# GpSimd's product with C written in place over the states, in one ring of six, and the skip one slot earlier

## The chip, the cores and the metric

The kernel runs on one core of one Trainium2 chip. The metric is the device time of one execution in microseconds (us); its time is given as the median of three runs. The engines are named PE (TensorE), DVE (VectorE), ACT (ScalarE), POOL (GpSimd) and SP (SyncE, which only issues transfers here).

## The reference, cut to what matters

The network has two layers on 16 images of 48 channels and 64 x 64 pixels. Layer 0 is a depthwise convolution with a routed expert and a feed-forward block; layer 1 masks the pixels, takes a 2D cosine transform, runs a selective scan on each of four quadrants, transforms back, and ends with a feed-forward block. The change touches the selective scan alone:

```python
xi = silu(conv(xi) + conv_b)                       # 96 channels d, 1024 positions l
delta = softplus(dt @ dt_w + dt_b)
dA = exp(delta[..., None] * A)                     # 16 states s per channel
dBu = delta[..., None] * Bm[:, :, None, :] * xi[..., None]
def step(h, inp):
    dA_t, dBu_t, C_t = inp
    h = dA_t * h + dBu_t
    return (h, jnp.einsum('bds,bs->bd', h, C_t))
y = ys + xi * Dp                                   # the skip
y = y * silu(z)                                    # the gate
out = jnp.einsum('bld,cd->blc', y, out_w)
```

(Shortened; `dt`, `Bm` and `Cm` come from `xi` by a matrix product, and `ys` are the results of `step` over the positions.)

## The kernel before

The 16 images are worked on in 8 pairs, one after the other. In a pair the scan has 8 units `v` (4 quadrants times 2 images), and a unit has 12 slots `m`. In a slot, 8 channels times 16 states make 128 partitions, and 1024 positions lie along the free axis, so a step is one instruction of 128 x 1024 on each engine. Each engine's program is written out by hand: `scan_stage` calls `step(v, m)` for a slot and then `prep(m, v + 1)`, which prepares the next unit. An engine runs its own list strictly in this order, and semaphores tie the engines together.

For slot `m` of a unit the work is:

- PE, `broadcast_u` (L625, L626): copies `u` = delta * xi to the 128 partitions in PSUM, into one of two bank pairs. It is issued one slot ahead and waits until the scan two slots back has read its banks (`h_ready`).
- ACT, `decay` (L875): dA = exp(A * delta), two slots ahead, in a ring of three (`da`).
- DVE, the mult (L1143): `driven` = broadcast u * B, in place in PSUM. Then the scan (L1148): h = dA * h + driven along the positions, from PSUM and `da` into `hs`, a ring of two. The scan waits until POOL has read the state of two slots back (`pr_ready`).
- POOL, the product (L1229): state * C from `hs` into `pr`, a ring of four (`PRS`). It waits for the scan (`h_ready`) and until PE has read the ring's slot (`y_acc`).
- PE, `states` (L644): once for three slots (a trio), six matmuls add three products into the sum y in PSUM. Trios 0, 1 and 2 are added in slots 4, 7 and 10, trio 3 in slot 1 of the next unit.

PE's list also holds, once per unit: `skip` (L636, xi * D with a diagonal matrix, which opens the sum y and so stands ahead of trio 0; it waits for the gate of the unit before, `yz_ready`) in slot `S_SKIP`; XI (L584) in slot 0, Z (L592) in slot 2, DT (L598) in slot 3, B (L604) in slot 5, C (L610) in slot 7, all for the next unit; and every second unit the output projection (L654) in slot 9. DT's result goes through five activations on ACT (the first at L842, the last, a logarithm, at L851, with a `decay` among them). DVE turns it into delta by one add of two SBUF operands (the delta add, L1125) after the scan of slot 5. POOL then multiplies u (L1218). DVE's gate (L1133) follows the scan of slot 1.

The last unit of a pair prepares nothing, so it has neither DT nor delta add.

## Time and profile before

| | us |
|---|---|
| median of 3 runs | 5493.2 |
| lowest and highest of the 3 | 5470.5 and 5499.7 |
| profiled execution | 5469.5 |
| its span, first to last instruction | 5467.7 |
| PE busy | 4310.0 (79%) |
| DVE busy | 3967.0 (73%) |
| ACT busy | 2693.4 (49%) |
| POOL busy | 2379.3 (44%) |

The mean granted clock of TensorE is 0.786 of full speed. The eight pairs look alike, each about 683 us, of which the scan takes a little under 400 us. In these DVE is nearly always busy; in the rest of a pair it is not. A share of busy time over the whole span is therefore no guide to the change: what counts is which engine ends a wait last inside the scan.

### The profile page before, as it was taken

To read this page: it belongs to the slowest core of one execution; us is meant where nothing else is said; L and a number is where in the kernel's file an instruction comes from. 1 tells how busy PE (TensorE), PEld (TensorE's weight loads), DVE (VectorE), ACT (ScalarE), POOL (GpSimd) and SP (SyncE) were. 2 spreads that over 40 slices of the span, in tenths; PEclk is the share of its full clock that TensorE was granted. 3 is DMA by queue.
4 is the path that set the end of the run, shared out by engine and by line. 5 is a ranking of instruction groups with operands and counts; after the bars stand their busy time and mean duration, and the time that the engine had idled before them with its cause. 6 is when DMAs were issued, how large, how long until landed. Compare 5 with 4: busy or idle time off the path is not lost.

```text
span 5467.7 us, 47969 instructions
## 1 busy us (share of the span) xinstructions
PE 4310.0 (79%) x13448; PEld 1540.4 (28%) x13448; DVE 3967.0 (73%) x3477; ACT 2693.4 (49%) x3114; POOL 2379.3 (44%) x1148
## 2 busy tenths in 40 slices
PE   6688776887768877688776897768977688777887
PEld 2322323223232233322333223322233222332223
DVE  6588675886758866588665886658866588675886
ACT  4554355543555535555355554555535545355453
POOL 2256332563326533265333653326633266333663
PEclk8778787787878887777877778778887778877787
DMA  1355303553036520355203552036520366204651
GB/s 34 76 141 145 79 13 77 141 144 77 13 83 144 143 73 10 91 145 135 71 10 91 145 141 67 8 89 146 145 64 8 91 152 142 64 4 101 150 142 47
DMA packets 144739, 497.37 MB, mean 91 GB/s; under 512 B 19308, under 2 KB 20056, under 8 KB 143672
## 3 DMA queue, kind: packets, MB, share of 16 engines
q1 hardware_dynamic: 130104, 456.13, 34.5%
q10 hardware_dynamic: 14336, 37.76, 2.5%
q8 instruction: 126, 2.06, 0.2%
q14 instruction: 173, 1.42, 0.1%
HBM read 418.33 MB, written 37.75 MB: 83 GB/s over the span
## 4 chain that ended last, share of the span: by engine, by line
PE 34%; issue 25%; DVE 24%; ACT 8%; POOL 6%; DMA 2%; DVEq 1%; SPq 0%; POOLq 0%; ACTq 0%
DVE arena L1148 7%; DVE ps L1143 7%; PE ps L625 6%; PE ps L644 6%; POOL arena L1229 5%; PE ps L584 5%; DVE arena L1039 3%; PE ps L489 3%; PE ps L654 3%; PE ps L437 2%; PE ps L535 2%; PE ps L430 2%; ACT arena L731 2%; PE ps L480 2%; ACT arena L709 2%
## 5 line engine op out<-in xcount | busy, mean ns | idle before, releaser
L1229 POOL TENSOR_TENSOR arena<-arena 128x1024 f32<-128x1024 f32 x768 | 1804.0, 2358 | 1317.8 <-PE ps L644 848.8
L1148 DVE TENSOR_TENSOR_SCAN arena<-arena,ps 128x1024 f32<-128x1024 f32 x768 | 1756.3, 2287 | 120.4 <-ACT arena L875 17.9
L625 PE MATMUL ps<-arena,spread 32*128 32x512 f32 x1536 | 1009.9, 748 | 455.3 <-DVE arena L1148 429.0
L875 ACT ACTIVATE arena<-arena,a_all 128x1024 f32<-128x1024 f32 x768 | 869.3, 1144 | 973.6 <-DVE arena L1148 892.4
L1143 DVE TENSOR_TENSOR ps<-ps,arena 128x1024 f32<-128x1024 f32 x768 | 931.8, 1213 | 269.3 <-PE ps L626 267.9
L626 PE MATMUL ps<-arena,spread 32*128 32x512 f32 x1536 | 979.9, 748 | 0.0
L644 PE MATMUL ps<-arena,gather 128*32 128x512 f32 x3072 | 694.6, 814 | 38.4 <-POOL arena L1229 38.4
L625 PEld LDWEIGHTS ps<-arena,spread 32*128 32x128 f32 x1536 | 261.2, 209 | 1173.8 <-DVE arena L1148 769.2
L1177 POOL TENSOR_TENSOR x<-x,arena 96x512 f32<-96x512 f32 x128 | 204.2, 1595 | 862.4 <-DVE arena L957 862.4
L584 PE MATMUL ps<-arena,w_in 96*96 96x512 f32 x512 | 312.4, 767 | 63.0 <-DMA arena<-xq 63.0
L644 PEld LDWEIGHTS ps<-arena,gather 128*32 128x32 f32 x3072 | 126.5, 136 | 579.1 <-issue 528.8
L515 PE MATMUL ps<-arena 96*96 96x512 f32 x384 | 198.5, 666 | 69.7 <-DVE arena L1025 69.7
L626 PEld LDWEIGHTS ps<-arena,spread 32*128 32x128 f32 x1536 | 250.9, 208 | 0.0
L437 PE MATMUL ps<-arena,average 96*96 96x512 f32 x384 | 222.8, 664 | 29.7 <-ACT arena L702 29.7
L1125 DVE TENSOR_TENSOR arena<-arena 96x1024 f32<-96x1024 f32 x64 | 79.1, 1237 | 219.6 <-ACT arena L851 219.6
L636 PE MATMUL ps<-arena,dskip 96*96 96x512 f32 x256 | 229.8, 1051 | 0.0
L1218 POOL TENSOR_TENSOR arena<-arena 96x1024 f32<-96x1024 f32 x64 | 151.2, 2362 | 167.2 <-DVE arena L1125 167.2
L1039 DVE SCALAR_TENSOR_TENSOR arena<-arena,sel_small 96x512 f32<-96x512 f32 x192 | 217.1, 1131 | 6.6 <-DVE arena L1025 2.1
L469 PE MATMUL ps<-arena,w 128*96 128x512 fp8e5 x384 | 120.8, 429 | 125.5 <-DVE arena L932 113.0
L598 PE MATMUL ps<-arena,wdt_all 96*96 96x512 f32 x256 | 207.3, 957 | 5.5 <-ACT arena L834 5.5
L1190 POOL TENSOR_TENSOR arena<-arena 96x512 f32<-96x512 f32 x64 | 92.6, 1446 | 245.2 <-ACT arena L767 245.2
L731 ACT ACTIVATE arena<-ps 128x1536 f16<-128x1536 f32 x128 | 183.8, 1436 | 26.6 <-PE ps L459 26.6
(151 smaller groups left out, 5566.7 us busy)
## 6 DMA issues: line engine op xcount, KB each, us to landing
arena<-dl SPq DMA_DIRECT2D x768, 512.0 KB, 4.8
dl<-arena ACTq DMA_DIRECT2D x64, 384.0 KB, 3.0
xq<-in_x SPq DMA_DIRECT2D x8, 1536.0 KB, 8.8
arena<-xq SPq DMA_DIRECT2D x64, 192.0 KB, 7.4
arena<-arena ACTq DMA_DIRECT2D x64, 192.0 KB, 3.7
out<-x SPq DMA_DIRECT2D x64, 192.0 KB, 2.1
arena<-xq SPq DMA_DIRECT2D x64, 191.8 KB, 6.5
arena<-in_w SPq DMA_DIRECT2D x2, 288.0 KB
```

The lines of the kernel that those rows point to most:

```text
L437: pe.matmul(ps[0:R, depth + j % depth, :], average[:], sq[:, j % depth, :], start=True, stop=True).then_inc(averaged, 1)
L584: mm = pe.matmul(ps[0:DI, 6 + c, :], w_in[:, q, j, :], xs[:, i, c * 512 + 2 * j:c * 512 + 2 * j + 512], start=(j == 0), stop=(j == 1))
L625: pe.matmul(ps[:, bank, :], spread[rows[0], r, :], u[rows[0], i, 0:512], start=True, stop=True)
L626: mm = pe.matmul(ps[:, bank + 1, :], spread[rows[1], r, :], u_low[rows[1], i, :], start=True, stop=True)
L636: pe.matmul(ps[0:DI, c, :], dskip[:, q, :], xi[:, i, c * 512:(c + 1) * 512], start=True, stop=False, skip_group_check=True)
L644: mm = pe.matmul(ps[b * BLK:(b + 1) * BLK, c, :], gather[:, r, :], pr[:, (r * TRIO + b) % PRS, c * 512:(c + 1) * 512], start=False, stop=( ...
L731: act.activation(hf[:, j % 2, :], ps[:, 4:7, :].rearrange("p b n -> p (b n)"), ACT.Copy).then_inc(hf_ready, 1)
L875: act.activation(da[:, m % DAS, :], dbc[:, m % DBC, :], ACT.Exp, scale=a_all[:, v // 2, m:m + 1]).then_inc(da_ready, 1)
L1039: dve.scalar_tensor_tensor(out=image(acc), in0=tap_source(t, k), scalar=sel_small[:, k:k + 1], in1=image(acc), op0=ALU.mult, op1=ALU.add). ...
L1143: dve.tensor_tensor(driven, driven, bmat[:, v % 2, :], ALU.mult).then_inc(bu_ready, 1)
L1148: dve.tensor_tensor_scan(hs[:, m % 2, :], da[:, m % DAS, :], driven, 0.0, ALU.mult, ALU.add).then_inc(h_ready, 1)
L1229: pool.tensor_tensor(pr[:, m % PRS, :], hs[:, m % 2, :], cmat[:, v % 2, :], ALU.mult).then_inc(pr_ready, 1)
```

## The change

The ring `pr` is gone and `hs` has six slots (the same space as two and four before). POOL multiplies the state by C in place. PE's `states` reads its three products from `hs`. POOL no longer waits for PE; DVE's scan, which now must not overwrite a product that PE has still to read, waits for the trio that holds the slot six steps back (`y_acc`) in place of POOL's product two steps back. Apart from this, `S_SKIP` goes from 4 to 3, so `skip` stands in slot 3, ahead of DT, and not in slot 4.

```diff
--- before.py
+++ after.py
@@ -50,14 +50,14 @@
 TRIO = 3
 DBC = 3
 DAS = 3
-PRS = 4
+HSS = 6
 XSW = L + 2
 PE_XI, PE_Z, PE_DT, PE_B, PE_C = 0, 2, 3, 5, 7
 ACT_SILU, ACT_DT, ACT_SOFT, ACT_B, ACT_DL, ACT_C, ACT_U = 1, 3, 4, 6, 6, 8, 8
 DVE_DELTA = 5
 POOL_U = 5
 SP_SHIFT = 5
-S_GATE, S_SKIP, S_OUT = 1, 4, 9
+S_GATE, S_SKIP, S_OUT = 1, 3, 9
 ACT_TAPS, DVE_TAPS, PE_TAPS = (0, 1, 2), (3, 4, 5), (6, 7, 8)
 LN_DEPTH = 4
 ARENA = 30300
@@ -186,8 +186,7 @@
         u_low = cut(128, 2 * 512).rearrange("p (i n) -> p i n", i=2)
         dbc = cut(128, DBC * L).rearrange("p (b n) -> p b n", b=DBC)
         da = cut(128, DAS * L).rearrange("p (b n) -> p b n", b=DAS)
-        hs = two_of(cut(128, 2 * L))
-        pr = cut(128, PRS * L).rearrange("p (b n) -> p b n", b=PRS)
+        hs = cut(128, HSS * L).rearrange("p (b n) -> p b n", b=HSS)
         assert top[0] <= ARENA, top[0]
 
         ps = ctx.enter_context(nc.psum_tensor("ps", [128, 8, 512], F32))
@@ -642,7 +641,7 @@
                     for c in range(2):
                         for b in range(TRIO):
                             mm = pe.matmul(ps[b * BLK:(b + 1) * BLK, c, :], gather[:, r, :],
-                                           pr[:, (r * TRIO + b) % PRS, c * 512:(c + 1) * 512],
+                                           hs[:, (r * TRIO + b) % HSS, c * 512:(c + 1) * 512],
                                            start=False, stop=(r == GPB - 1), skip_group_check=True)
                     mm.then_inc(y_acc, 1)
 
@@ -1142,10 +1141,10 @@
                     dve.wait_ge(ubc_ready, n + 1)
                     dve.tensor_tensor(driven, driven, bmat[:, v % 2, :], ALU.mult).then_inc(bu_ready, 1)
                     dve.wait_ge(da_ready, n + 1)
-                    if v or m >= 2:
-                        dve.wait_ge(pr_ready, n - 1)
+                    if v or m >= HSS:
+                        dve.wait_ge(y_acc, V * GPB + (m - HSS) // TRIO + 1)
                     dve.wait_ge(bu_ready, n + 1)
-                    dve.tensor_tensor_scan(hs[:, m % 2, :], da[:, m % DAS, :], driven, 0.0,
+                    dve.tensor_tensor_scan(hs[:, m % HSS, :], da[:, m % DAS, :], driven, 0.0,
                                            ALU.mult, ALU.add).then_inc(h_ready, 1)
                     if m == S_GATE and v:
                         gate(v - 1)
@@ -1224,9 +1223,8 @@
                     if m == 0:
                         pool.wait_ge(c_ready, V + 1)
                     pool.wait_ge(h_ready, n + 1)
-                    if v or m >= PRS:
-                        pool.wait_ge(y_acc, V * GPB + (m - PRS) // TRIO + 1)
-                    pool.tensor_tensor(pr[:, m % PRS, :], hs[:, m % 2, :], cmat[:, v % 2, :],
+                    product = hs[:, m % HSS, :]
+                    pool.tensor_tensor(product, product, cmat[:, v % 2, :],
                                        ALU.mult).then_inc(pr_ready, 1)
 
                 scan_stage(prep, lambda: None, step, lambda: None)
```

PE's list at slots 3 to 5 of a unit, from broadcast 4 to broadcast 6, where `spread` is the broadcast, `wdt_all` DT, `dskip` the skip and `gather` states of trio 0. Before:

```order
L625 MATMUL ps<-arena,spread 128x512 [waits h_ready]
L626 MATMUL ps<-arena,spread 128x512
L598 MATMUL ps<-arena,wdt_all 96x512 [waits sz_ready]
L598 MATMUL ps<-arena,wdt_all 96x512
L623 REGISTER_ALU
L625 MATMUL ps<-arena,spread 128x512 [waits h_ready]
L626 MATMUL ps<-arena,spread 128x512
L636 MATMUL ps<-arena,dskip 96x512 [waits yz_ready]
L636 MATMUL ps<-arena,dskip 96x512
L641 ISA
L644 MATMUL ps<-arena,gather 32x512 [waits pr_ready]
L644 MATMUL ps<-arena,gather 32x512 x5
```

The same place after the change:

```order
L624 MATMUL ps<-arena,spread 128x512 [waits h_ready]
L625 MATMUL ps<-arena,spread 128x512
L635 MATMUL ps<-arena,dskip 96x512 [waits yz_ready]
L635 MATMUL ps<-arena,dskip 96x512
L597 MATMUL ps<-arena,wdt_all 96x512 [waits sz_ready]
L597 MATMUL ps<-arena,wdt_all 96x512
L622 REGISTER_ALU
L624 MATMUL ps<-arena,spread 128x512 [waits h_ready]
L625 MATMUL ps<-arena,spread 128x512
L640 ISA
L643 MATMUL ps<-arena,gather 32x512 [waits pr_ready]
L643 MATMUL ps<-arena,gather 32x512 x5
```

The two skip matmuls have moved ahead of DT and of broadcast 5; the rest stands as it did, and the next row in both lists is broadcast 6.

DVE's list around slots 5 and 6, with the mult, the scan (printed as SCALAR_TENSOR_TENSOR) and between them the delta add. Before:

```order
L1143 TENSOR_TENSOR ps<-ps,arena 128x1024 [waits ubc_ready]
L1148 SCALAR_TENSOR_TENSOR arena<-arena,ps 128x1024 [waits bu_ready,pr_ready,da_ready]
L1124 ISA
L1125 TENSOR_TENSOR arena<-arena 96x1024 [waits soft_act]
L1142 REGISTER_ALU
L1143 TENSOR_TENSOR ps<-ps,arena 128x1024 [waits ubc_ready]
L1148 SCALAR_TENSOR_TENSOR arena<-arena,ps 128x1024 [waits bu_ready,pr_ready,da_ready]
```

After:

```order
L1142 TENSOR_TENSOR ps<-ps,arena 128x1024 [waits ubc_ready]
L1147 SCALAR_TENSOR_TENSOR arena<-arena,ps 128x1024 [waits bu_ready,y_acc,da_ready]
L1123 ISA
L1124 TENSOR_TENSOR arena<-arena 96x1024 [waits soft_act]
L1141 REGISTER_ALU
L1142 TENSOR_TENSOR ps<-ps,arena 128x1024 [waits ubc_ready]
L1145 REGISTER_ALU [waits da_ready]
L1147 SCALAR_TENSOR_TENSOR arena<-arena,ps 128x1024 [waits bu_ready,y_acc]
```

The scan waits for `y_acc` in place of `pr_ready`. At some scans, 23 in a pair's list in place of 7, a register instruction now stands ahead of the scan and carries one of its waits. No other engine's list differs, but POOL's, where the products lose their wait for `y_acc`.

## Rows read from the trace of the kernel before

**Rows 1.** Page, costliest groups; then the scan's line, its idle time behind POOL.

```profile
L1229 POOL TENSOR_TENSOR arena<-arena 128x1024 f32<-128x1024 f32 x768 | 1804.0, 2358 | 1317.8 <-PE ps L644 848.8
L1143 DVE TENSOR_TENSOR ps<-ps,arena 128x1024 f32<-128x1024 f32 x768 | 931.8, 1213 | 269.3 <-PE ps L626 267.9
...
  POOL arena L1229: 11.0, 54
```

**Rows 2.** Timeline of DVE, second unit of the third pair (start, length).

```profile
1649.54 2.29 DVE L1148 TENSOR_TENSOR_SCAN arena<-arena,ps 128x1024 f32<-128x1024 f32 x1
...
1659.14 1.23 DVE L1143 TENSOR_TENSOR ps<-ps,arena 128x1024 f32<-128x1024 f32 x1 [0.23 <-PE ps L626]
1660.51 2.29 DVE L1148 TENSOR_TENSOR_SCAN arena<-arena,ps 128x1024 f32<-128x1024 f32 x1
1662.71 1.20 DVE L1125 TENSOR_TENSOR arena<-arena 96x1024 f32<-96x1024 f32 x1
1667.39 1.23 DVE L1143 TENSOR_TENSOR ps<-ps,arena 128x1024 f32<-128x1024 f32 x1 [3.48 <-PE ps L626]
1668.83 2.29 DVE L1148 TENSOR_TENSOR_SCAN arena<-arena,ps 128x1024 f32<-128x1024 f32 x1 [0.21 <-POOL arena L1229]
```

**Rows 3.** Timeline of PE, same unit, first row of each group.

```profile
1651.88 0.69 PE L625 MATMUL ps<-arena,spread 32*128 32x512 f32 x1 [1.94 <-DVE arena L1148]
...
1653.36 3.73 PE L598 MATMUL ps<-arena,wdt_all 96*96 96x512 f32 x4
1657.02 1.22 PE L625 MATMUL ps<-arena,spread 32*128 32x512 f32 x1
...
1659.03 3.73 PE L636 MATMUL ps<-arena,dskip 96*96 96x512 f32 x4
1662.68 3.60 PE L644 MATMUL ps<-arena,gather 128*32 128x512 f32 x12
```

**Rows 4.** Timelines of POOL and ACT, same unit.

```profile
1651.91 2.36 POOL L1229 TENSOR_TENSOR arena<-arena 128x1024 f32<-128x1024 f32 x1 [2.40 <-DVE arena L1148]
...
1657.13 1.11 ACT L842 ACTIVATE arena<-ps,small_all 96x1024 f32<-96x1024 f32 x1 [3.06 <-PE ps L598]
...
1661.25 1.15 ACT L851 ACTIVATE arena<-arena,eps 96x1024 f32<-96x1024 f32 x1
```

**Rows 5.** Windows, same unit: busy by engine, then granted clock, DMA share, GB/s.

```profile
1656.00:1666.00 10.00, 10.00 (x22) 2.05 (x20) 7.41 (x5) 7.32 (x7) 1.79 (x1) 0.50 0.88 190
```

**Rows 6.** Timelines of DVE and PE, fourth unit of the same pair.

```profile
1751.05 2.29 DVE L1148 TENSOR_TENSOR_SCAN arena<-arena,ps 128x1024 f32<-128x1024 f32 x1
...
1763.40 2.74 PE L644 MATMUL ps<-arena,gather 128*32 128x512 f32 x12
...
1767.24 1.23 DVE L1143 TENSOR_TENSOR ps<-ps,arena 128x1024 f32<-128x1024 f32 x1 [2.17 <-PE ps L626]
```

**Rows 7.** Timelines of DVE and POOL, delta adds of two units at full speed.

```profile
1615.08 1.45 DVE L1125 TENSOR_TENSOR arena<-arena 96x1024 f32<-96x1024 f32 x1
1616.46 1.22 DVE L1143 TENSOR_TENSOR ps<-ps,arena 128x1024 f32<-128x1024 f32 x1
...
5210.74 5.66 POOL L1229 TENSOR_TENSOR arena<-arena 128x1024 f32<-128x1024 f32 x2 [3.68 <-PE ps L644]
5211.63 2.56 DVE L1125 TENSOR_TENSOR arena<-arena 96x1024 f32<-96x1024 f32 x1
```

**Rows 8.** Timelines: first and last wait at slot 6; broadcast 5 of the last.

```profile
255.43 1.23 DVE L1143 TENSOR_TENSOR ps<-ps,arena 128x1024 f32<-128x1024 f32 x1 [2.33 <-PE ps L626]
...
5354.66 1.22 PE L625 MATMUL ps<-arena,spread 32*128 32x512 f32 x1 [1.47 <-DVE arena L1148]
...
5364.53 1.23 DVE L1143 TENSOR_TENSOR ps<-ps,arena 128x1024 f32<-128x1024 f32 x1 [2.84 <-PE ps L626]
```

**Rows 9.** Timelines of DVE and POOL, end of the third pair's scan.

```profile
1984.03 2.29 DVE L1148 TENSOR_TENSOR_SCAN arena<-arena,ps 128x1024 f32<-128x1024 f32 x1
1984.42 4.64 POOL L1229 TENSOR_TENSOR arena<-arena 128x1024 f32<-128x1024 f32 x2 [2.77 <-PE ps L644]
```

## Prediction

> **What bounds the kernel now.** I read the groups of instructions first. The change touches two of them: POOL's product (L1229), which stands idle 848.8 us behind PE's `states` (L644), and DVE's `mult` (L1143), which stands idle 267.9 us behind PE's `broadcast_u` (L626) [rows 1]. Which of the two idle times matters is settled by DVE's timeline of one unit [rows 2]. A step of DVE is one mult and one scan. Inside the step nothing is left over, and in the whole scan stage DVE only stops where PE or a unit's start stops it. The stops are concentrated: of the 267.9 us, 158.7 us fall on the mult of slot 6, in 59 of 64 units (the first and the last of the 59 are in [rows 8]; the sum is over all of them). POOL's idle time costs nothing by itself: the one place where DVE waits for a product is the scan of slot 6, 0.21 us of idle in [rows 2], 54 times, 11.0 us in all [rows 1].
>
> So the question is what delays slot 6, and PE's timeline of the same unit answers it [rows 3]. From 1651.88 on PE never pauses: broadcast 4, DT, broadcast 5, skip, states 0, broadcast 6. The granted clock in this stretch is 0.50, the lower level of 1.2 GHz [rows 5], after a slot in which PE was idle 1.94 us [rows 3]. PE is therefore the bound between broadcast 4 and broadcast 6, and DVE is the bound everywhere else. POOL's product 4 waits here for states 0, because its slot in the ring of four is still being read: waits of this kind make up the 848.8 us of [rows 1].
>
> **The change part by part.** *The ring.* DVE's scan now waits for `y_acc` of the trio six steps back in place of POOL's product two steps back. Slot 6 waits for states 0, but its mult already needs broadcast 6, which PE issues behind states 0 (order rows of PE). The same holds at slots 9, 0 and 3. The new wait can never end last, so it costs 0. What it gives is the scan of slot 6. Its start comes 1.44 us after a mult that itself waited; the scan of slot 5 in the same unit starts 1.37 us after such a mult [rows 2]. That is 0.07 us, 54 times: -4 us. At the end of a pair the scan of the last slot starts at 1984.03 and POOL's last two products run as one piece from 1984.42 to 1989.06 [rows 9]. A product starts 2.37 us after its scan's start when nothing else holds it (1649.54 to 1651.91 [rows 2, 4]) and takes 2.36 us [rows 4], so the last one would end at 1988.76: -0.3 us on the path to the last gate, eight times, -3 us with rounding. Sixteen more register instructions per pair stand on DVE between mult and scan. One stands ahead of almost every mult already and the delta add starts 2.20 us after a scan of 2.29 us [rows 2]: they hide behind the running instruction, 0. An in-place product reads and writes what it did; I take its 2.36 us unchanged, and even 1.1 us more would fit into the 3.5 us of a step: 0.
>
> *The skip.* It takes 3.73 us at the low clock [rows 3] and moves ahead of DT and broadcast 5. PE's total is unchanged, but broadcast 5 now ends where states 0 starts today. Mult 5 follows 0.11 us later (1659.03 to 1659.14 [rows 2, 3]). From mult 5 DVE needs 1.37 us to scan 5, 2.20 us to the delta add [rows 2] and 1.13 us to mult 6 (an add takes 1.20 us and the next mult starts 0.07 us before its end: 1615.08 + 1.45 against 1616.46 [rows 7]). So mult 6 cannot start before (start of states today) + 0.11 + 4.70 us. Today the wait at mult 6 has mult 5, scan 5 and the add running beneath it; after the change they stand behind the wait. This is the step on which the forecast rests. I went through all 64 units with it.
> - 24 units like the one in [rows 2, 3]: 1662.68 + 4.81 = 1667.49 against 1667.39. This one loses 0.1, their mean is 0.3 us: +7.
> - 27 units like the one in [rows 6], where PE was back at full speed within states 0 (2.74 us in place of 3.60): 1763.40 + 4.81 = 1768.21 against 1767.24, +0.97, mean 1.0: +27 as the lower bound. In these the clock rose right behind a skip, with the first matmuls of states. In the new order DT and broadcast 5 stand ahead of states, and in none of the 64 units does it rise on broadcasts. If the rise is as late as in the first group, mult 6 comes where it does there, 17.85 us after scan 2 starts, not 16.19 [rows 2, 6]: +1.7 each, +45, the upper bound. Nearer the upper one, 1.35: +36.
> - 5 units at or near full speed: mult 6 hardly waits today. DT comes one skip later and the delta add may be late (rival 1): between -0.3 (today's 1.45 us of the add falls to 1.20 [rows 7]) and +2.3 each (2.5 us less that 0.25), middle: +5.
> - 8 last units of a pair, without DT and delta add. PE idles 1.47 us ahead of broadcast 5, which the skip now fills, out of a wait of 2.84 us at mult 6 [rows 8]: -1.4 each if the clock stays, -0.7 if states run wholly at 3.6 us. I take -1: -8.
>
> Sum: +7 + 36 + 5 - 8 - 4 - 3 = **+33 us**. The profiled execution took 5469.5 us, so 5502 us for such a one. It lies 24 us under the median of the runs shown, 5493.2; on the median the forecast is **5526 us**.
>
> **Rivals.** *1. The delta add loses to POOL's product (slower still).* Today product 5 waits behind product 4 for states 0, so the delta add of slot 5 mostly runs alone. In the full-speed units it doesn't, and there it takes 1.45 us, once 2.56 us in place of 1.20, while the two products around it take 5.66 us in place of 4.7 [rows 7]: whichever starts second waits for the other to end. After the change product 5 becomes ready 0.17 us behind the add's turn (2.37 against 2.20 us after scan 5 starts [rows 2, 4]). The add must be ready by then. Its logarithm ends 5.27 us after DT's first evaluation starts, 0.31 us before the add [rows 2, 4]; both hang on DT and broadcast 5, so at the low clock the 0.31 us stay. If broadcast 5 runs at full speed right behind DT, it ends 1 us sooner: the add isn't ready, the product goes first and the add comes 0.17 + 2.36 = 2.5 us later. In a third of the 51 units of the first two kinds that is 17 x 2.5 = +43 us: 5569; in all of them +128: 5654. The point where it decides is 0.31 + 0.17 us of slack. The Trainium skill, "SBUF — State Buffer", section "Who interferes with whom", states the rule behind it: a VectorE instruction with two SBUF inputs contends with a GpSimd instruction that reads SBUF, and the one that issued first blocks the other for its whole length. The mult and the scan have one input in PSUM and are clear of it by that page. Trace and rule agree: the scans take 2.29 us beside a product (1984.03) and without one (1660.51) [rows 2, 9].
>
> *2. Nothing changes.* PE's work between broadcasts 4 and 6 is the same sum, and if the stop only changes its place the time stays within 10 us: 5493. For it: mult 6 moves by 0.1 us in the unit of [rows 2]. Against it: [rows 6].
>
> *3. PE keeps its full speed (faster).* The skip fills PE's idle time between broadcast 4 and broadcast 5. If the clock then stayed up as in the five full-speed units, today's wait at mult 6 would go: 3.48 us in the one kind of unit, 2.17 us in the other [rows 2, 6], 2.8 us on the mean of the 51. In half of them that is -71 us, with the +33 us falling away by half: 5493 + 17 - 71 = 5439. It decides when more than about 17 of the 51 do so. Against it: the clock falls on what PE did before broadcast 4, which the change leaves alone, and a fast broadcast 5 runs into rival 1.
>
> *4. The change does not do what it says* is out: the order rows show both parts.
>
> **How the numbers follow.** Forecast (stop moves ahead of mult 5, 5505 to 5545): 0.60. Rival 1 in a third of the units or more (5550 to 5650): 0.17. Rival 2 (5483 to 5503): 0.13. Rival 3: 0.10. A difference under 0.5%, 27 us, is about what a measurement of this kernel can't tell from none (the three runs shown spread by 29 us). The edge stands at 5521: six tenths of the forecast's chance lie above it. Slower 0.36 + 0.17 = 0.53; same 0.24 + 0.13 = 0.37; faster 0.10. The range leaves out 0.10 below and the far half of rival 1: 5480 to 5580.
>
> **What would show it.** Idle before the mult of slot 6 falls from 158.7 us to near 40 us, and a new idle of 2 to 4 us stands before the mult of slot 5 in some 50 units, 180 us or more in all. POOL's product no longer waits for states at all, and the scan never waits for POOL. The unit grows by 0 to 2 us from scan 2 to mult 6. If rival 1 holds, the delta add (L1124 after) has a mean above 1.5 us or waits for ACT outside the pair's start. If rival 3 holds, the granted clock of the span rises above 0.79. The forecast is wrong if the idle before slots 5 and 6 together falls, or if the clock's low stretches end inside DT rather than states.

## The result, and the profile after

The changed kernel takes **5549.95 us** (median of 4 runs, 5540.98 to 5567.24) against 5487.2 us for the kernel before in the same comparison (4 runs, 5470.54 to 5499.65). The ratio is 1.0115, 95% interval 1.0085 to 1.0146: 63 us slower. The forecast was +33 us. The profiled execution took 5567.24 us, with a span of 5565.4 us against 5467.7. That is the slowest of the four runs after, and the profiled execution of before, 5469.5 us, lies 18 us under its median. So sums read from the two traces account for 98 us, 35 more than the medians differ by.

First the groups of the page, as in [rows 1].

```profile
L1227 POOL TENSOR_TENSOR arena<-arena 128x1024 f32<-128x1024 f32 x768 | 1807.5, 2354 | 1401.0 <-DVE arena L1147 1401.0
L1147 DVE TENSOR_TENSOR_SCAN arena<-arena,ps 128x1024 f32<-128x1024 f32 x768 | 1755.8, 2286 | 107.4 <-ACT arena L874 13.3
...
L1142 DVE TENSOR_TENSOR ps<-ps,arena 128x1024 f32<-128x1024 f32 x768 | 932.2, 1214 | 284.5 <-PE ps L625 282.6
...
L1124 DVE TENSOR_TENSOR arena<-arena 96x1024 f32<-96x1024 f32 x64 | 173.4, 2710 | 251.3 <-ACT arena L850 251.3
```

The product costs what it did (2354 ns against 2358), and no longer waits for PE at all. The scan's wait for POOL is gone. DVE's wait for broadcasts is hardly changed as a sum, 282.6 us against 267.9. What is new stands in the last row: the delta add has a mean of 2.71 us, where the kernel before had 1.24 us (79.1 us busy in 64), and it waits 251.3 us for the logarithm, of which 217.9 us are the eight adds at the pairs' starts, as before (219.6).

DVE's timeline shows it in the fifth unit of the third pair. 46 of the 56 units with such an add look like it; the second unit, that of [rows 2], is one of ten others: its wait ahead of mult 5 is 0.51 us in place of 2.15, its add is the same.

```profile
1843.98 2.29 DVE L1147 TENSOR_TENSOR_SCAN arena<-arena,ps 128x1024 f32<-128x1024 f32 x1
1848.42 1.23 DVE L1142 TENSOR_TENSOR ps<-ps,arena 128x1024 f32<-128x1024 f32 x1 [2.15 <-PE ps L625]
1849.79 2.29 DVE L1147 TENSOR_TENSOR_SCAN arena<-arena,ps 128x1024 f32<-128x1024 f32 x1
1852.66 2.93 DVE L1124 TENSOR_TENSOR arena<-arena 96x1024 f32<-96x1024 f32 x1 [0.59 <-ACT arena L850]
1855.52 1.22 DVE L1142 TENSOR_TENSOR ps<-ps,arena 128x1024 f32<-128x1024 f32 x1
```

The stop now stands ahead of mult 5 (2.15 us) and none ahead of mult 6. The add comes 0.59 us late and takes 2.93 us in place of 1.20. PE's timeline of the same stretch (as [rows 3]) says why it is late.

```profile
1840.90 3.73 PE L635 MATMUL ps<-arena,dskip 96*96 96x512 f32 x4
1844.42 2.90 PE L597 MATMUL ps<-arena,wdt_all 96*96 96x512 f32 x4
1847.25 0.69 PE L624 MATMUL ps<-arena,spread 32*128 32x512 f32 x1
...
1848.31 1.92 PE L643 MATMUL ps<-arena,gather 128*32 128x512 f32 x12
...
1859.18 1.21 PE L624 MATMUL ps<-arena,spread 32*128 32x512 f32 x1 [4.93 <-DVE arena L1147]
```

The skip runs at the low clock (3.73 us, as before), but DT, now right behind it, takes 2.90 us in place of 3.73, and broadcast 5 takes 0.69 us in place of 1.22. The windows over the same unit (granted clock third from the end, as in [rows 5]) have the rise from 1.2 to 2.4 GHz between 1846 and 1850; by the length of DT it falls into DT's last matmuls.

```profile
1840.00:1843.00 3.00, 3.00 (x7) 0.96 (x4) 2.87 (x3) 1.42 (x2) 1.82 (x2) 0.50 0.44 131
1843.00:1846.00 3.00, 3.00 (x4) 0.85 (x3) 2.87 (x2) 0.00 (x0) 2.15 (x1) 0.50 1.01 225
1846.00:1850.00 4.00, 4.00 (x19) 0.98 (x17) 1.71 (x3) 2.65 (x3) 2.35 (x1) 0.94 0.47 95
```

ACT and POOL there (as [rows 4]):

```profile
1847.36 1.11 ACT L841 ACTIVATE arena<-ps,small_all 96x1024 f32<-96x1024 f32 x1 [5.93 <-PE ps L597]
...
1851.48 1.15 ACT L850 ACTIVATE arena<-arena,eps 96x1024 f32<-96x1024 f32 x1
...
1852.15 2.36 POOL L1227 TENSOR_TENSOR arena<-arena 128x1024 f32<-128x1024 f32 x1 [3.46 <-DVE arena L1147]
```

The logarithm ends at 1852.63. Product 5 starts at 1852.15, before it, and ends at 1854.51. The add ends 1.08 us after that: it ran only once the product was through. This is rival 1 of the prediction. The same holds in all 56 units that have such an add outside a pair's start: the adds take 2.89 to 2.93 us.

I added up DVE's idle time ahead of each slot from the rows of all 64 units, and the length of the eight scan stages, from the start of a pair's first scan to the end of its last. The row "the rest" is the span less those. Labels are those of the experiments below.

| us | before | after | e1 | e2 | e3 | e4 | e5 | e6 | e7 | e9 |
|---|---|---|---|---|---|---|---|---|---|---|
| idle, mult 5 | 12.3 | 128.5 | 6.4 | 53.6 | 87.7 | 104.8 | 16.7 | 0 | 107.0 | 0 |
| idle, mult 6 | 158.7 | 12.1 | 156.0 | 3.2 | 8.6 | 11.3 | 222.8 | 0.9 | 2.9 | 1.9 |
| idle, mult 9 | 22.0 | 66.1 | 10.3 | 112.7 | 101.1 | 1.1 | 3.1 | 29.3 | 81.8 | 113.9 |
| idle, gate in slot 1 | 85.1 | 107.7 | 114.2 | 188.5 | 152.8 | 72.5 | 98.5 | 130.3 | 158.5 | 191.0 |
| idle, add (56 units) | 0 | 33.3 | 0 | 31.3 | 32.5 | 0 | 0 | 0 | 0 | 0 |
| add busy | 79.1 | 173.4 | 76.8 | 194.7 | 78.2 | 76.7 | 76.8 | 76.8 | 76.8 | 76.9 |
| scan stages | 3168.0 | 3316.2 | 3183.6 | 3378.3 | 3254.3 | 3047.1 | 3242.7 | 3013.5 | 3215.0 | 3160.2 |
| the rest | 2299.7 | 2249.2 | 2294.3 | 2303.4 | 2265.3 | 2247.3 | 2283.2 | 2273.7 | 2285.2 | 2238.6 |

The scan stages grew by 148 us: add 94.3, its wait 33.3, slots 5 and 6 together -30.4, mult 9 +44.1, the gate +22.6, and smaller ones (scan 6 -10.9, mult 11 from 17.3 to 0) that take the sum to 136, and with mults 0, 2 and 4 to 154, of which a part of mult 0 lies outside the stages. The rest shrank by 50 us, for which the prediction had 3. It comes behind the last scan of each pair. PE's timeline there, the first pair of before and then of after, from the last `states` on:

```profile
630.66 3.63 PE L644 MATMUL ps<-arena,gather 128*32 128x512 f32 x12 [4.80 <-POOL arena L1229]
635.63 6.88 PE L654 MATMUL ps<-arena,wo 96*96 96x512 f32 x8 [1.33 <-DVE arena L1133]
```

```profile
648.86 3.35 PE L643 MATMUL ps<-arena,gather 128*32 128x512 f32 x12 [3.86 <-POOL arena L1227]
653.55 3.67 PE L653 MATMUL ps<-arena,wo 96*96 96x512 f32 x8 [1.34 <-DVE arena L1132]
```

and the windows of both from 5 us behind the start of the pair's last scan (625.64 and 644.11), before and then after:

```profile
630.64:640.64 10.00, 8.64 (x18) 2.39 (x19) 1.22 (x1) 0.00 (x0) 0.00 (x0) 0.50 0.00 0
640.64:650.64 10.00, 8.03 (x52) 6.45 (x51) 4.17 (x8) 2.62 (x2) 0.00 (x0) 0.76 0.00 0
```

```profile
649.11:659.11 10.00, 6.77 (x20) 1.60 (x14) 1.22 (x1) 1.85 (x1) 0.00 (x0) 0.87 0.00 0
659.11:669.11 10.00, 9.85 (x96) 9.63 (x96) 3.80 (x8) 6.17 (x8) 0.00 (x0) 1.00 0.01 2
```

Before, PE sat idle 4.80 us ahead of the last `states`, and what follows ran for some 15 us at 1.2 GHz, the projection among it. After, the pause is 3.86 us and the granted clock is 2.4 GHz from the projection on: 3.67 us in place of 6.88. From the last scan of a pair to the first of the next is 284.4 us before and 275.7 us after in these two pairs; over the seven such stretches it is 47 us less, 2.5 to 9.0 us each.

Of the 0.94 us by which the pause is shorter, 0.3 us are the ring's. The last `states` starts 5.03 us after the last scan in the pair shown of before, 4.97 to 5.10 us in all eight, and 4.76 us in every pair of every kernel with the ring. The other 0.7 us are PE's: its last work ahead of the pause ends 0.90 us after the last scan's start, not 0.23.

### The profile page after: what moved, and what is told of

Read it like the earlier page. It is cut to its first block, busy times and chain, and to the rows that moved or that the text cites. A ratio compares the mean times of both kernels' runs of the same rounds, so it can differ in the third digit from the quotient of the medians.

```text
span 5565.4 us, 47361 instructions
## 1 busy us (share of the span) xinstructions
PE 4220.2 (76%) x13448; PEld 1536.7 (28%) x13448; DVE 4057.6 (73%) x3477; ACT 2688.5 (48%) x3114; POOL 2391.8 (43%) x1148
## 4 chain that ended last, share of the span: by engine, by line
POOL 33%; issue 29%; PE 18%; DVE 9%; ACT 7%; DMA 3%; POOLq 0%; SPq 0%; DVEq 0%; ACTq 0%
POOL arena L1227 30%; DVE arena L1038 3%; PE ps L488 2%; POOL arena L1217 2%; PE ps L436 2%; PE ps L534 2%; PE ps L429 2%; ACT arena L708 1%; ACT arena L730 1%; PE ps L479 1%; DMA arena<-dl 1%; PE ps L514 1%; PE ps L468 1%; PE ps L583 1%; ACT arena L701 1%
## 5 line engine op out<-in xcount | busy, mean ns | idle before, releaser
L1227 POOL TENSOR_TENSOR arena<-arena 128x1024 f32<-128x1024 f32 x768 | 1807.5, 2354 | 1401.0 <-DVE arena L1147 1401.0
L624 PE MATMUL ps<-arena,spread 32*128 32x512 f32 x1536 | 1038.8, 770 | 653.8 <-DVE arena L1147 619.5
L1142 DVE TENSOR_TENSOR ps<-ps,arena 128x1024 f32<-128x1024 f32 x768 | 932.2, 1214 | 284.5 <-PE ps L625 282.6
L625 PE MATMUL ps<-arena,spread 32*128 32x512 f32 x1536 | 979.0, 775 | 0.0
L643 PE MATMUL ps<-arena,gather 128*32 128x512 f32 x3072 | 679.4, 798 | 30.9 <-POOL arena L1227 30.9
L624 PEld LDWEIGHTS ps<-arena,spread 32*128 32x128 f32 x1536 | 274.1, 218 | 1325.4 <-DVE arena L1147 943.3
L1124 DVE TENSOR_TENSOR arena<-arena 96x1024 f32<-96x1024 f32 x64 | 173.4, 2710 | 251.3 <-ACT arena L850 251.3
L625 PEld LDWEIGHTS ps<-arena,spread 32*128 32x128 f32 x1536 | 254.8, 218 | 0.3
L841 ACT ACTIVATE arena<-ps,small_all 96x1024 f32<-96x1024 f32 x64 | 71.1, 1110 | 321.1 <-PE ps L597 321.1
```

The costliest lines, as they stand in the source:

```text
L624: pe.matmul(ps[:, bank, :], spread[rows[0], r, :], u[rows[0], i, 0:512], start=True, stop=True)
L625: mm = pe.matmul(ps[:, bank + 1, :], spread[rows[1], r, :], u_low[rows[1], i, :], start=True, stop=True)
L643: mm = pe.matmul(ps[b * BLK:(b + 1) * BLK, c, :], gather[:, r, :], hs[:, (r * TRIO + b) % HSS, c * 512:(c + 1) * 512], start=False, stop=( ...
L1142: dve.tensor_tensor(driven, driven, bmat[:, v % 2, :], ALU.mult).then_inc(bu_ready, 1)
L1227: pool.tensor_tensor(product, product, cmat[:, v % 2, :], ALU.mult).then_inc(pr_ready, 1)
```

## The experiments

All were timed beside the kernel before, in three groups, in which that kernel's median was 5486.17 us (e1 to e4), 5494.47 us (e5 to e8) and 5487.98 us (e9 to e12). Each ratio is to the kernel before of its own group; a difference in us between kernels of different groups carries such an offset. Below, e1, e2 and so on stand for the labels.

### The two parts alone: e1_ring_only and e2_skip_only

e1 is the changed kernel with one number back:

```diff
-S_GATE, S_SKIP, S_OUT = 1, 3, 9
+S_GATE, S_SKIP, S_OUT = 1, 4, 9
```

> The ring of six and the product in place, with the skip back in slot 4. Theory A (the cost comes from the skip's place: broadcast 5 runs at full speed right behind DT, the delta add is ready about 0.6 us too late and stands behind product 5 in 56 units): the clock rises behind the skip as before, the add is ready before product 5 and takes 1.20 us in most units, the scan no longer waits for a product; 5480 us, within 15 us of the kernel before. Theory B (the ring itself costs, by the product in place or by product 5 coming at once): slower than before by 40 us or more, with adds of 2.9 us.

Measured: 5481.96 us, ratio 0.9983 (0.9966 to 1.0000). All 56 adds are back at 1.20 us, none waits, and the wait at mult 6 is 156.0 us, as before. That is Theory A. The interval allows a gain of 0 to 19 us: alone, the ring costs nothing that shows, and its gain is at the edge of what can be told from none.

e2 is the kernel before with only the skip moved:

```diff
-S_GATE, S_SKIP, S_OUT = 1, 4, 9
+S_GATE, S_SKIP, S_OUT = 1, 3, 9
```

> The skip in slot 3, with the two rings of before. Theory A: the wait moves from the mult of slot 6 to that of slot 5 as in the changed kernel, and the add comes late by 0.6 us; product 4 waits for states 0 and ends about when the add gets ready, so the add may go ahead of product 5 or behind it: 10 to 75 us slower than before. Theory B: no more than 10 us from before.

Measured: 5700.48 us, ratio 1.0394 (1.0363 to 1.0425), far above what either theory had given. POOL and DVE of one unit show one reason why it is worse than both parts together.

```profile
1765.09 4.68 POOL L1229 TENSOR_TENSOR arena<-arena 128x1024 f32<-128x1024 f32 x2 [3.52 <-PE ps L644]
...
1767.43 3.43 DVE L1125 TENSOR_TENSOR arena<-arena 96x1024 f32<-96x1024 f32 x1 [0.59 <-ACT arena L851]
```

With the old ring of four, product 4 still waits for `states`. Product 5 follows it without a pause, at 1767.42, and the add, ready at 1767.43, has the whole of product 5 ahead of it, until 1769.77. It ends 1.09 us after that: 3.43 us in place of 2.93, in 53 of the 56 units. This is the smaller part. Of the 116 us between the spans of e2 and the changed kernel the longer adds are 21; the gate waits 81 us more and mult 9 47 us more, mults 5 and 6 wait 84 us less, and the rest is 54 us longer, with a pause of 4.80 us at each pair's end. The skip's new place is what costs, and the ring takes some 150 us of that cost away (5700 against 5550). The two parts do not add up; a theory that prices them apart misses it.

### The collision by itself: e3_product_after_add

The changed kernel, with product 5 made to wait for the add:

```diff
+                    if m == DVE_DELTA and v + 1 < UNITS:
+                        pool.wait_ge(delta_ready, V + 2)
```

> The changed kernel, where POOL's product of slot 5 also waits for the delta add. Theory A: the add takes 1.20 us again in all units and comes 0.6 us late as now; 56 x 1.73 = 97 us less than the changed kernel, about 5455 us, which would be some 30 us faster than before. Theory C (the long add is covered, and the growth is the moved stop alone): within 15 us of the changed kernel.

Measured: 5526.65 us, ratio 1.0077 (1.0049 to 1.0106), 23 us under the changed kernel. Theory A had 5455 us, so its time is missed, though its adds came as it said.

```profile
1830.59 1.22 DVE L1124 TENSOR_TENSOR arena<-arena 96x1024 f32<-96x1024 f32 x1 [0.59 <-ACT arena L850]
...
1844.45 1.23 DVE L1142 TENSOR_TENSOR ps<-ps,arena 128x1024 f32<-128x1024 f32 x1 [2.02 <-PE ps L625]
...
1831.95 2.34 POOL L1229 TENSOR_TENSOR arena<-arena 128x1024 f32<-128x1024 f32 x1 [5.32 <-DVE arena L1124]
```

The add takes 1.22 us with the product behind it and 2.93 us with the product ahead, everything else alike: the collision is shown to be the cause of the long add. All 64 adds are between 1220 and 1224 ns. The Trainium skill, "SBUF — State Buffer", section "Who interferes with whom", states this rule, that of a VectorE instruction with two SBUF inputs and a GpSimd instruction that reads SBUF the first to issue blocks the other. The changed kernel bears it out with the product first; the other order is seen in e4 below, where the product behind the add takes 3.25 us in place of 2.36.

But of the 95 us that the adds gave back the kernel kept only a part. The table shows where they went: 41 more came off mult 5, and 35 us went to mult 9 and 45 us to the gate; the scan stages fell by 62, and the rest rose by 16. In time, then, the collision accounts for 23 of the 63 us; the other 40 us are still there in e3. PE in this unit (broadcast 8, `states`, C):

```profile
1835.39 1.21 PE L624 MATMUL ps<-arena,spread 32*128 32x512 f32 x1 [3.22 <-DVE arena L1147]
...
1837.40 3.63 PE L643 MATMUL ps<-arena,gather 128*32 128x512 f32 x12
1840.96 2.38 PE L609 MATMUL ps<-arena,xp_rep 96*128 96x512 f32 x4
```

PE waits 3.22 us for the scan of slot 6, which stands behind the add, and comes back at 1.2 GHz: `states` takes 3.63 us and C 2.38, and mult 9 waits 2.02 us for broadcast 9. Broadcast 8 starts at 1.2 GHz in all 56 units of e3, as it does in the changed kernel.

### The add in another slot: e4, e5, e8

e4_add_slot6 is the changed kernel with the add and POOL's u behind slot 6; broadcast 8 then waits for a scan that stands ahead of the add.

```diff
-DVE_DELTA = 5
-POOL_U = 5
+DVE_DELTA = 6
+POOL_U = 6
```

> The changed kernel, where the delta add stands behind the scan of slot 6 and u behind product 6, one slot later each. Theory A: the add is ready long before its turn, so it starts 0.17 us ahead of product 6 and takes 1.20 us, and the wait of 0.6 us for ACT goes too: 56 x 2.3 = 130 us less than the changed kernel, about 5420 us. Theory C: within 15 us of the changed kernel. What could eat the gain: delta and u reach the next unit one slot later, and its first broadcast or decay would wait.

Measured: 5338.96 us (5296.17 to 5373.69), ratio 0.9729 (0.9703 to 0.9755), 211 us under the changed kernel, where Theory A had 130. The profiled execution, of which the table is, was the fastest, 43 us under the median. DVE's add, POOL's product 6 and PE's broadcast 8 and `states` in one unit:

```profile
1813.67 1.20 DVE L1124 TENSOR_TENSOR arena<-arena 96x1024 f32<-96x1024 f32 x1
...
1813.84 3.25 POOL L1227 TENSOR_TENSOR arena<-arena 128x1024 f32<-128x1024 f32 x1 [1.15 <-DVE arena L1147]
...
1813.81 0.70 PE L624 MATMUL ps<-arena,spread 32*128 32x512 f32 x1 [1.39 <-DVE arena L1147]
...
1815.31 3.12 PE L643 MATMUL ps<-arena,gather 128*32 128x512 f32 x12
```

PE pauses 1.39 us where it paused 4.93, broadcast 8 starts at full speed (in 55 of 56 units), and the add now stands over the time in which PE gets broadcast 9 ready: mult 9 waits 1.1 us in all, not 66.1. The add starts 0.17 us ahead of product 6, so now the product is the one that waits, which costs DVE nothing.

Two kernels with the skip back in slot 4 separate the add's slot from the skip's. e5_ring_skip4_add6:

```diff
-S_GATE, S_SKIP, S_OUT = 1, 3, 9
+S_GATE, S_SKIP, S_OUT = 1, 4, 9
-DVE_DELTA = 5
-POOL_U = 5
+DVE_DELTA = 6
+POOL_U = 6
```

> The ring of six, the skip in slot 4, the delta add and u one slot later. Theory A2 (the skip ahead of DT lets PE reach full speed within DT, which is worth more than it costs once the add is out of the way): broadcast 5 stays at low clock as in the ring-only kernel, so this keeps the wait at slot 6 of about 2.4 us less up to 1.2 us, as the add no longer stands in front of mult 6; between the ring-only kernel and 20 us below it, 5460 to 5485 us. Theory D (the add's slot alone makes the gain): near 5340 us.

and e8_before_add6, the kernel before with the same two numbers at 6:

> The kernel before (two rings, skip in slot 4) with the delta add and u one slot later. Theory A2: up to 20 us faster than before, as the add no longer stands between scan 5 and mult 6 but mult 6 waits for broadcast 6 anyway; the add may run into POOL's products 4 and 5, which start late, up to 2.4 us in some units: 5450 to 5500. Theory D (the add's slot alone makes the gain): near 5340.

Measured: e5 5537.66 us, ratio 1.0075 (1.0052 to 1.0097); e8 5539.48, ratio 1.0073 (1.0050 to 1.0096). Both theories miss in both: a slower kernel was in neither. DVE's timeline, e1 and then e5, at slots 5 and 6:

```profile
1663.42 1.20 DVE L1124 TENSOR_TENSOR arena<-arena 96x1024 f32<-96x1024 f32 x1
1668.27 1.23 DVE L1142 TENSOR_TENSOR ps<-ps,arena 128x1024 f32<-128x1024 f32 x1 [3.64 <-PE ps L625]
```

```profile
1682.92 1.23 DVE L1142 TENSOR_TENSOR ps<-ps,arena 128x1024 f32<-128x1024 f32 x1 [3.28 <-PE ps L625]
1684.26 2.29 DVE L1147 TENSOR_TENSOR_SCAN arena<-arena,ps 128x1024 f32<-128x1024 f32 x1
1686.46 1.20 DVE L1124 TENSOR_TENSOR arena<-arena 96x1024 f32<-96x1024 f32 x1
```

With the skip in slot 4 the stop is at mult 6, and an add ahead of it is free: it lies over the wait. Behind slot 6 it is not. The sum of the wait at mult 6 rises by 66.8 us from e1 to e5, that is 1.1 us in each of some 60 units, the length of an add. The unit shown is not one of those in which it rises (3.28 us against 3.64); it rises by more than 0.5 us in 46 of the 56, most often from 2.17 us. The add belongs ahead of the stop, or, if the stop stands earlier, ahead of the next one.

### The skip in slot 2: e6, e9, e10

e6_ring_skip2_add6 is e4 with one more number changed:

```diff
-S_GATE, S_SKIP, S_OUT = 1, 3, 9
+S_GATE, S_SKIP, S_OUT = 1, 2, 9
```

> As the kernel with add in slot 6, with the skip one more slot ahead, in slot 2, behind broadcast 3 and ahead of Z. PE's 1.9 us of idle time ahead of broadcast 4 is then filled in part by the skip (it must wait for the gate), and slots 3 and 4 hold less. Theory A2: the wait at slot 5 (105 us) falls by half or more and the clock falls less often ahead of broadcast 4; 5270 to 5340 us. Rival: Z comes later, so does the SiLU pair on ACT and with it DT, and the time goes up to 5400.

Measured: **5270.77 us**, ratio 0.9580 (0.9554 to 0.9607), the fastest of all and 224 us under the kernel before in the same group. It lies in Theory A2's range. The stop at mults 5 and 6 is gone. The page and the groups of lines of e6 for the mult and the gate:

```profile
L1142 DVE TENSOR_TENSOR ps<-ps,arena 128x1024 f32<-128x1024 f32 x768 | 929.7, 1211 | 111.6 <-PE ps L625 110.4
...
L1132 DVE TENSOR_TENSOR arena<-ps,arena 96x1024 f32<-96x1024 f32 x64 | 78.1, 1221 | 178.5 <-PE ps L643 178.5
```

The mult waits 111.6 us in place of 269.3 [rows 1]; the gate is now the larger wait.

e9_ring_skip2 is e6 with the add and u back in slot 5:

```diff
-DVE_DELTA = 6
-POOL_U = 6
+DVE_DELTA = 5
+POOL_U = 5
```

> The ring of six with the skip in slot 2 and the delta add left in slot 5. In the kernel with skip 2 and the add in slot 6, DT follows broadcast 4 directly and broadcast 5 waits for its scan, as it did in the kernel before at full speed. Theory A: the add of slot 5 is then ready about in time; if it is ready less than 0.17 us behind its turn it costs nothing, so the time lies near the kernel with skip 2 and add 6, 5270 to 5330 us, with adds of 1.20 us. If ready later, product 5 goes first in most units, the adds take up to 3.5 us and the time is 5400 us or more.

Measured: 5409.01 us, ratio 0.9851 (0.9812 to 0.9890), some 80 us over the range given for adds of 1.20 us. The adds are at 1.20 us and none waits in the middle units, so no collision is left and the second branch, late adds, is not what made the time; yet the scan stages are 147 us longer than e6's, with 85 us at mult 9 and 61 us at the gate. The add's slot has a price of its own, apart from the port. PE pauses 3.5 us in the mean ahead of broadcast 8, which starts at 1.2 GHz in all 56 units; in e6 the pause is 2.4 us and it does so in 28.

e10_rings_skip2_add6 is the kernel before with skip in slot 2 and add and u in slot 6, so e6 with the old two rings:

> The two rings of before, with the skip in slot 2 and the add in slot 6: the ring of six taken away from the fastest kernel so far (5271 us). Theory A: with the skip out of slots 3 and 4, states 0 come right behind broadcast 5, so product 4 waits for them 3 us or so and product 5 runs behind it; the add of slot 6 may meet product 5 or 6 in the port. Between 5271 and 5400 us: the ring is worth 0 to 130 us here. Rival (the ring of six is worth nothing): within 15 us of 5271.

Measured: 5333.63 us, ratio 0.9719 (0.9695 to 0.9743). Its scan stages take 3011.9 us against 3013.5 in e6. In the scan the ring is worth nothing here, whereas with the skip in slot 3 and the add in slot 5 it was worth 62 us (e2 against the changed kernel). The medians lie 63 us apart, the profiled executions 40 us, and these differ behind the pairs' last scans, by 42 us. e10's windows there, from 5 us behind the start of the first pair's last scan:

```profile
611.06:621.06 10.00, 8.00 (x18) 2.25 (x19) 1.22 (x1) 0.00 (x0) 0.62 (x1) 0.53 0.00 0
621.06:631.06 10.00, 8.03 (x45) 7.05 (x44) 4.43 (x8) 1.88 (x1) 0.00 (x0) 0.66 0.00 0
```

In the first pair of e6 the same two have 0.87 and 1.00, like the changed kernel. That holds in four of e6's eight pairs, those with a pause of 3.86 or 3.87 us; in the others it is 4.19 to 4.22 us, and the clock 0.56 and 0.66. In all pairs of e10 the pause is 4.80 us, and the last `states` starts 5.7 us after the last scan where e6 has 4.76; that is 0.9 us a pair, 7 of the 42 us.

### DT ahead of the skip: e7_dt_then_skip

The changed kernel, with the skip called right behind DT, in the same slot:

```diff
                         mm.then_inc(dt_ready, 1)
+                        if v:
+                            skip(v - 1)
...
-                    if m == S_SKIP:
+                    if m == S_SKIP and v + 1 == UNITS:
```

> The changed kernel with the skip still in slot 3 but behind DT, not ahead of it. The add stays in slot 5. The add is then ready some 2 to 3 us before its turn. Theory A: it takes 1.20 us, ACT's wait goes, PE pauses about 2 us less ahead of broadcast 8 and keeps full speed there; near the kernel with the add in slot 6, 5340 us, within 30. Rival (the skip in slot 3 is bad whatever the add does): above 5480.

Measured: 5495.02 us, ratio 0.9998 (0.9984 to 1.0011), 55 us under the changed kernel and no more than that. Theory A, 5340 us, is missed; the time is the rival's. All that the change had lost is back, and the clock now rises within the skip in all 56 units. The adds are at 1.20 us and don't wait, so the add's 130 us (97 busy, 33 of waiting) all came back, and 31 us at mults 5 and 6; the gate took 51 us and mult 9 another 16, and the rest is 36 us longer than in the changed kernel.

### What is left: e11_xi_slot1 and e12_b_three_times

e11 is e6 with XI one slot later, so that `states` of the unit before, on which the gate waits, would not stand behind it:

```diff
-PE_XI, PE_Z, PE_DT, PE_B, PE_C = 0, 2, 3, 5, 7
+PE_XI, PE_Z, PE_DT, PE_B, PE_C = 1, 2, 3, 5, 7
```

> The fastest kernel so far (ring, skip 2, add 6; 5271 us) with XI moved from slot 0 to slot 1, behind states of trio 3. The gate then no longer waits for XI and its wait of 130 us falls to 20 to 50 us. Theory: 40 to 100 us faster, 5170 to 5230. Rival: XI and Z come later, ACT's SiLU pair holds back the decays and DT, and a new wait at slot 4 or 5 eats it: 5260 or more.

Measured: 5413.87 us, ratio 0.9862 (0.9838 to 0.9887), 143 us slower than e6: the theory is missed and the rival came. The gate gives 7.6 us; mult 4 now waits 55.2 us, the scan of slot 4 waits 44.2 us for `decay` and mult 3 waits 33.1 us.

e12 is the changed kernel with B's two matmuls issued three times (the last pass gives the result), to fill PE's pause ahead of broadcast 8:

```diff
-                        for c in range(2):
+                        for c in (0, 1) * 3:
```

> The changed kernel, with B's two matmuls in slot 5 done three times over (same values written again, 3.8 us more work for PE at full speed in a stretch where it stands idle 4.9 us ahead of broadcast 8). Theory E (part of the loss is PE's low clock behind that pause: broadcast 8 starts at the low clock in all middle units, and mult 9 waits 66 us, the gate 108 us): broadcast 8 runs at full speed, mult 9 waits under 20 us, the gate less too, and the kernel gets 30 to 80 us faster for more work. Rival (the pause costs nothing, these waits have another cause): same time or up to 50 us slower, since B comes later.

Measured: 5627.43 us, ratio 1.0253 (1.0224 to 1.0283), 77 us slower than the changed kernel, and slower than the rival's 50 us too. PE at broadcast 8 and `states`, and DVE's mult 9 of the same unit:

```profile
1822.40 0.69 PE L624 MATMUL ps<-arena,spread 32*128 32x512 f32 x1 [1.50 <-DVE arena L1147]
...
1823.46 3.57 PE L643 MATMUL ps<-arena,gather 128*32 128x512 f32 x12
...
1830.05 1.23 DVE L1142 TENSOR_TENSOR ps<-ps,arena 128x1024 f32<-128x1024 f32 x1 [0.62 <-PE ps L625]
```

Broadcast 8 now starts at full speed in 42 of 56 units, but in the unit shown the clock falls right behind it, within `states`. Mult 9 still waits 55.9 us in all, and the gate's wait grows from 107.7 us to 174.5. That the pause ahead of broadcast 8 alone makes the waits at mult 9 and the gate is not borne out: with it filled, the low stretch came a few us later. The adds are as long as ever (170.3 us busy), and the scan stages too (3318.6 us against 3316.2): of the 55 us between the two spans 53 lie outside the scan, which I did not follow further.

## Why the prediction was right or wrong

- **The ring.** Its steps came as foretold: the new wait for `y_acc` never ends last, the scan of slot 6 no longer waits (11.0 us to 0), the product in place costs 2.35 us, and the last `states` of a pair starts 0.3 us sooner. The size isn't shown: forecast -7, e1 against before -4 by the medians (5481.96 against 5486.17 us), with an interval from 0 to -19, while in the profiled execution of e1 the scan stages are 16 us longer than before and the rest 5 us shorter.
- **The stop moves from mult 6 to mult 5.** Right: 158.7 us to 12.1, and 12.3 to 128.5. It was foretold as 180 us or more. Together the two fell by 30 us, which the prediction had named as a sign against itself. Its other such sign, a low stretch that ends inside DT, came too, in all 56 units.
- **The step that failed** is the one on the clock: DT and broadcast 5 stand ahead of `states`, "in none of the 64 units does it rise on broadcasts", so mult 6 would come as late as in the first group. The rows of before had shown the rise behind a skip only with `states`, because there `states` came next; I read from that that it needed `states`. Behind skip and DT in a row it rose within DT. The reading was also wrong as it stood: in seven of the 64 units of before, all with mult 6 at 17.8 us after scan 2, the granted clock rose within broadcast 6 (in the fifth unit of the third pair 0.50 from 1814.0 to 1816.2 and 1.00 from 1816.4). The distance from scan 2 to mult 6, over the 56 units with an add, shows what the early rise did. Its mean was 16.83 us before (17.85 in the unit of [rows 2], 16.19 in that of [rows 6]). The forecast had it grow by 48 us over the units of these three kinds, 0.9 each. It is 18.79 us in the changed kernel, 1.96 more (110 us in all), and 16.25 us in e3, where the product stands behind the add. Less the 128 us that the late and longer adds put into it, the 110 us are -18 us; by e3 the three terms, +7, +36 and +5, would have come out near -32 us. Without the collision their sign was wrong, not only their size.
- **Rival 1 was the mechanism,** and the prediction had tied it to just this: if broadcast 5 runs fast behind DT, the 0.31 us of slack are gone. It was priced at 2.5 us a unit; it measured 1.7 us of longer add and 0.6 us of waiting, 2.3 us, in 56 of 56 units, 128 us. The chance of 0.17 for a third of the units or more was too low: once the clock rose in DT, all units had the late add (46 of the 56 take 18.6 us from scan 2 to mult 6). For all units the rival's time was 5654 us, 104 us above what was measured: its mechanism held and its sum did not.
- **What the sum didn't have:** +44 us at mult 9 and +23 us at the gate, and -50 us behind the pairs' last scans, where I had counted 0.3 us a pair for a product that ends sooner and not what PE's shorter pause does to its clock. The time, 5550 us, lies within the range given, 5480 to 5580, though above the 5505 to 5545 of the forecast's own mechanism. That is luck: losses that the sum didn't have, the late adds above all, and a gain of 50 us that it didn't have either, came out near a small positive number.
- **Rival 2** is out: the interval, 1.0085 to 1.0146, lies clear of 1. **Rival 3** came in part. Its sign, a granted clock above 0.79, was met, 0.791 to 0.795 in the four runs against 0.786 in the profiled execution of before, and broadcast 5 ran at full speed. Its gain did not come, since the fast broadcast 5 ran into rival 1, as the prediction had said of it.

What is shown: the skip ahead of DT is what costs (e1 and e7 are back at the time of before), and the collision is 23 us of it (e3). What stays open is why 40 us remain in e3 at mult 9 and at the gate, and 147 us in e9 against e6. The rows name a companion: broadcast 8 starts at 1.2 GHz in all 56 units of the changed kernel, e2, e3 and e9, where PE's mean pause ahead of it is 4.9, 5.3, 3.2 and 3.5 us, in 28 to 36 units of e6, e7, e10 and e11 (2.4 and 2.5 us), and in 1 to 5 units of before, e1, e4, e5 and e8 (0.8 to 1.4 us). That removing PE's pause would cure the waits was tried and failed (e12). Which order of matmuls keeps the clock up at the gate was not found.

## What to carry to other kernels

Moving work on one engine moves the moment at which a neighbour's result arrives; where that result feeds an instruction with half a microsecond of slack against a competitor for the same memory, price the loss of the race in every unit, since a hand-written order makes all units lose or win together. Put a short side job on the busy engine ahead of the place where it waits anyway: with the stop at mult 6 the add in slot 5 was free, and with the stop at mult 5 it was free nowhere before slot 6 (e4 against the changed kernel, 211 us). And try neighbouring slots together: the add in slot 6 alone cost 45 us (e8), the skip in slot 3 alone 214 us (e2), the skip in slot 2 with the ring gave 1.5% (e9), and skip in slot 2 with the add in slot 6 gave 4.2% with the ring (e6) and 2.8% without it (e10).

## What was not expected of the hardware

- The granted clock can rise within four matmuls of DT that follow four of the skip, all 96x96 with 512 columns, both in PE's low stretch (DT 2.90 us, then broadcasts of 0.69 us). Before the change DT, broadcast 5 and the skip in the same stretch all ran at 1.2 GHz in most units [rows 3]; in one, the fifth of the eighth pair, DT began low and the clock was up again behind it (0.50 from 5202.4 to 5205.6, 1.00 from 5205.8). With DT first and the skip behind it, the rise fell within the skip (e7, 56 of 56 units).
- A shorter pause at a pair's end, 3.86 us in place of 4.80, went with a granted clock of 0.87 and 1.00 in the 20 us behind it in place of 0.50 and 0.76. The stretch between pairs was 2.5 to 9.0 us shorter. Over the 112 pair ends of the fourteen kernels, 38 have a pause of 3.85 to 3.88 us, and in 37 of them the mean granted clock of these 20 us is 0.93 or 0.94; 74 have one of 4.13 to 4.88 us, and there it is 0.59 to 0.73. That the pause is the cause wasn't tried by itself.
- A blocked add waits for the product that is running when its turn comes, not for one that stands behind it. In [rows 7] the add ends 1.08 us after the first of two products (5213.11) and the second goes behind the add, with 3.34 us in place of 2.36. Where it starts 0.5 us behind a product it takes 2.93 us, right behind one's start 3.43 us (e2).
